# Image stage with the softmax division on two engines and the maximum in two instructions; last stage with four buffers and whole rows (one core)

## The reference, cut to what matters

```python
att = jnp.einsum('bpqhd,bpkhd->bphqk', q_pix * SCALE, k_sel)     # 49 windows, 4 heads, 64 x 256
att = jax.nn.softmax(att, axis=-1)
o = jnp.einsum('bphqk,bpkhd->bpqhd', att, v_sel)
...
xr = mamba(conv(x).reshape(B * H * W, 8, 16)).reshape(B, C, H, W)
g = xr.reshape(B, 4, 32, H, W)
g = (g - g.mean((2, 3, 4))) / jnp.sqrt(g.var((2, 3, 4)) + 1e-5)
return x + silu(g.reshape(B, C, H, W) * gn_w + gn_b)
```

## Time and profile before

| | us |
|---|---|
| median of 3 runs (10958.4 to 10985.89) | 10985.12 |
| the profiled execution | 10976.78 |
| its span | 10974.7 |
| VectorE busy | 9186.9 (84%) |
| TensorE busy | 8590.6 (78%) |
| GpSimd busy | 6007.1 (55%) |
| ScalarE busy | 5945.0 (54%) |

### The profile page before, as it was taken

One profiled execution on the slowest core, in us unless ns is written; L12 is line 12 of the kernel. 1 busy time (PEld: TensorE's weight loads), 2 busy tenths in 40 slices (PEclk: granted clock), 3 DMA queues, 4 the chain that ended last, 5 costly groups with the idle time before them and its releaser, 6 DMA issues. The chain is left out here.

```text
span 10974.7 us, 195169 instructions
## 1 busy us (share of the span) xinstructions
PE 8590.6 (78%) x61658; PEld 3670.2 (33%) x61658; DVE 9186.9 (84%) x11368; ACT 5945.0 (54%) x10997; POOL 6007.1 (55%) x3646
## 2 busy tenths in 40 slices
PE   5888888888888888778777777788777777787850
PEld 3554544544444445222222222222222222222210
DVE  7777777777777777699999999999999999999974
ACT  4555555555555555555555555555555555555533
POOL 2222222222222222487788788887887877878750
PEclk9999999999999999888889898888898888889875
DMA  2222222222222222111111111111111111111139
GB/s 65 66 66 66 66 66 66 66 66 66 66 66 66 66 66 69 43 37 34 36 36 37 35 36 35 37 35 36 36 38 34 38 34 36 36 36 36 35 69 233
DMA packets 865726, 590.60 MB, mean 54 GB/s; under 512 B 622704, under 2 KB 725104, under 8 KB 860496
## 3 DMA queue, kind: packets, MB, share of 16 engines
q1 hardware_dynamic: 761424, 423.61, 17.0%
q0 software_dynamic: 49152, 100.76, 2.5%
q10 hardware_dynamic: 54016, 51.91, 1.6%
HBM read 109.27 MB, written 103.81 MB: 19 GB/s over the span
## 5 line engine op out<-in xcount | busy, mean ns | idle before, releaser
L1136 POOL TENSOR_TENSOR b_hh<-b_hh,b_cn 128x1024 f32<-128x1024 f32 x1600 | 3832.5, 2412 | 1034.3 <-DVE b_hh L1391 1033.4
L1391 DVE TENSOR_TENSOR_SCAN b_hh<-b_dA,b_ub 128x512 f32<-128x512 f32 x3200 | 3864.8, 1208 | 0.0
L1260 ACT ACTIVATE b_dA<-b_db,b_negA 128x448 f32<-128x448 f32 x3200 | 1976.6, 633 | 1736.0 <-PE b_db L1485 1717.8
L267 POOL DMA_DIRECT2D kvsel<-kv x1536 | 1103.0, 721 | 3188.5 <-issue 2408.6
L1383 DVE TENSOR_TENSOR b_ub<-b_ub,b_bn 128x512 f32<-128x512 f32 x3200 | 2173.0, 679 | 360.8 <-PE b_ub L1485 343.8
L1485 PE MATMUL b_ub<-b_rows,b_pick 96*64 96x512 bf16 x6400 | 1401.6, 439 | 988.1 <-DVE b_hh L1391 947.2
L1485 PE MATMUL b_db<-b_rows,b_pick 96*64 96x512 bf16 x6400 | 1266.0, 419 | 218.9 <-ACT b_dA L1260 215.5
L1485 PEld LDWEIGHTS b_ub<-b_rows,b_pick 96*64 96x64 bf16 x6400 | 358.4, 110 | 3172.6 <-DVE b_hh L1391 2523.7
L522 DVE SCALAR_TENSOR_TENSOR oacc<-vpad,vec,oacc 128x1064 f32<-128x1064 f32 (+1 forms) x934 | 1197.9, 1299 | 11.4
L383 ACT ACTIVATE prob<-score,nmax 128x256 f32<-128x256 f32 (+1 forms) x1600 | 735.5, 471 | 818.1 <-DVE nmax L493 726.9
L1521 PE MATMUL b_acc<-b_hh,b_gather 64*32 64x512 f32 x12800 | 1046.1, 716 | 2.8 <-POOL b_hh L1136 2.8
(11 more groups left out here) (179 smaller groups left out, 12057.2 us busy)
## 6 DMA issues: line engine op xcount, KB each, us to landing
b_rows<-b_term SPq DMA_DIRECT2D x2400, 64.0 KB, 2.0
kvsel<-kv SPq DMA_DIRECT2D x1600, 64.0 KB, 2.0
kvsel<-kv POOLq DMA_DIRECT2D x1536, 64.0 KB, 2.0
xpad<-in_x SPq DMA_DIRECT2D x18, 1568.0 KB, 10.6
ys<-ysb ACTq DMA_DIRECT2D x16, 1600.0 KB, 8.6
b_yc<-ys SPq DMA_DIRECT2D x100, 256.0 KB, 2.7
xr<-b_xo SPq DMA_DIRECT2D x100, 256.0 KB, 2.1
x<-x3pad SPq DMA_DIRECT2D x16, 1568.0 KB, 18.1
```

The lines of the kernel that those rows point to most:

```text
L267: eng.dma_start(kvsel[:, slot, j, :, WPIX * t:WPIX * (t + 1)].unsqueeze(1), kv[:, bass.ds(at[t], 1), :, :]).then_inc((s_kv, s_kg)[j][slot] ...
L1136: nc.gpsimd.tensor_tensor(out=now, in0=now, in1=cn[:, par, :].unsqueeze(1).broadcast_to([C, 2, HT]), op=ALU.mult).then_inc(s_pm, 1)
L1260: nc.scalar.activation(later(dA[:, k % DEEP, :]), later(db[k % 2][:, :]), ACT.Exp, scale=negA[:, 8 * q + e:8 * q + e + 1]).then_inc(s_a, 1)
L1391: nc.vector.tensor_tensor_scan(hh[:, k // 2 % PDEEP, HT * (k % 2):HT * (k % 2 + 1)], dA[:, k % DEEP, :], ub[(UNITS * par + k) % 3][:, :], ...
```

## The change

Image stage: `largest` becomes two instructions of two heads each, with a count of the semaphore for each; ScalarE's exponentials wait for the first before head 0 and for the second before head 2. VectorE divides heads 0 and 1; a new function `share` on ScalarE divides heads 2 and 3, by copies with a scale. `turned` is split in two, and the new function stands between the halves. TensorE's transposes wait for both engines. Sequence stage: `xr_dram` is laid out as (128, 4, 12800), so that `store` writes four pieces of 512 B a partition. Last stage: four buffers; xr comes in three loads of whole rows (12,288 B and 12,544 B, and one small); VectorE's body is cut in three, and the moments of image b+1 stand between the scales of image b and its addition.

```diff
@@ layer0, scalar
             def weights(b, p):
                 n, u = b * PAIRS + p, p % 2
-                act.wait_ge(s_m, ONE + n + 1)
                 if p >= 2:
                     act.wait_ge(s_pt, ONE + n - 1)
                 for h in range(HEADS):
+                    if h % 2 == 0:
+                        act.wait_ge(s_m, ONE + 2 * n + h // 2 + 1)
                     nc.scalar.activation(prob[rows(p), u, h], score[rows(p), h, 0:TOPK * WPIX], ACT.Exp,
...
+            def share(b, p):
+                n, u = b * PAIRS + p, p % 2
+                act.wait_ge(s_ri, ONE + n + 1)
+                for h in range(SHARED, HEADS):
+                    now = prob[rows(p), u, h]
+                    m = nc.scalar.activation(now, now, ACT.Copy, scale=rinv[rows(p), u, h:h + 1])
+                m.then_inc(s_ns, 1)
...
                 nc.scalar.activation(pT[:, u, :, rows(p)], turn[:, :, rows(p)], ACT.Copy).then_inc(s_pte, 1)
+            def kept(b, p):
+                n, u = b * PAIRS + p, p % 2
                 act.wait_ge(s_vt, ONE + n + 1)
+                if p >= 2:
+                    act.wait_ge(s_o, ONE + n - 1)
                 nc.scalar.activation(vT[:, u, 0:wins(p)].rearrange("k j c m -> k (j c m)"),
...
                         if p >= 1:
                             turned(b, p - 1)
+                        if p < PAIRS:
+                            share(b, p)
+                        if p >= 1:
+                            kept(b, p - 1)
@@ layer0, vector
-                nc.vector.tensor_reduce(out=nmax[rows(p), u], in_=score[rows(p), :, 0:TOPK * WPIX], axis=AXX, op=ALU.max,
-                                        negate=True).then_inc(s_m, 1)
+                for h in range(0, HEADS, 2):
+                    nc.vector.tensor_reduce(out=nmax[rows(p), u, h:h + 2], in_=score[rows(p), h:h + 2, 0:TOPK * WPIX],
+                                            axis=AXX, op=ALU.max, negate=True).then_inc(s_m, 1)
...
-                for h in range(HEADS):
+                for h in range(SHARED):
@@ layer0, tensor
                         pe.wait_ge(s_nm, ONE + n + 1)
+                        pe.wait_ge(s_ns, ONE + n + 1)
@@ sequences, sync
-                sp.dma_start(xr_dram[bass.ds(n, 1)].rearrange("a c g p -> c (a g) p"), xo[:, :, :]).then_inc(s_os, 16)
+                sp.dma_start(xr_dram[:, :, bass.ds(n * CPX, CPX)], xo[:, :, :]).then_inc(s_os, 16)
@@ normalise
-        S = 2
+        S = 4
...
-                sp.wait_ge(s_res, ONE + FREE + b - 1)
...
+                sp.wait_ge(s_res, ONE + FREE + b - (S - 1))
+                seq = xr_dram[:, g, bass.ds(q * SPX, SPX)]
+                sp.dma_start(xr[0:64, u, 0:PIX - WPIX], seq[0:64, 0:PIX - WPIX]).then_inc(s_x[u], 16)
+                sp.dma_start(xr[0:64, u, PIX - WPIX:PIX], seq[64:128, 0:WPIX]).then_inc(s_x[u], 16)
+                sp.dma_start(xr[64:128, u, :], seq[64:128, WPIX:SPX]).then_inc(s_x[u], 16)
...
+            moments(0, 0, 0)
+            with dve.Fori(0, NB - 1) as q:
+                for g in range(G):
+                    b = q * G + g
+                    scales(b, g)
+                    moments(b + 1, q + (g + 1) // G, (g + 1) % G)
+                    total(b, g)
```

More of the change, by code:

```diff
@@ L189, in layer0 @@
         s_nm = sem("s_nm")
+        s_ns = sem("s_ns")
         s_oa = sem("s_oa")
@@ L239, in layer0 @@
         GROUP = 4
+        SHARED = 2
         def places(k):
@@ L1622, in sem @@
             return sems[-1]
-        red = [ctx.enter_context(nc.psum_tensor(f"c_red{i}", [C, 2], FP32)) for i in range(2)]
-        S = 2
+        red = [ctx.enter_context(nc.psum_tensor(f"c_red{i}", [C, 2], FP32)) for i in range(4)]
+        S = 4
         vec = sb("vec", [C, NV])
@@ L1641, in normalise @@
         s_w = sem("w")
-        s_x = [sem("x0"), sem("x1")]
+        s_x = [sem(f"x{i}") for i in range(S)]
         s_st = sem("st")
@@ L1649, in normalise @@
         s_res = sem("res")
-        s_out = [sem("out0"), sem("out1")]
+        s_out = [sem(f"out{i}") for i in range(S)]
         def v(name):
             return vec[:, _V[name][0]:_V[name][0] + 1]
-        N_W, LOADS, STATS = 2, 6, 9
+        N_W, LOADS, STATS = 2, 5, 9
         FREE = S
@@ L1661, in images @@
                 for g in range(G):
-                    body(q * G + g, q, g, g % 2)
+                    body(q * G + g, q, g, g)
         @block.sync
@@ L1669, in body @@
             def body(b, q, g, u):
-                sp.wait_ge(s_res, ONE + FREE + b - 1)
-                chunk = xr_dram[bass.ds(q * CHUNKS, CHUNKS), :, g, :].rearrange("j c p -> c j p")
-                sp.dma_start(xr[0:64, u, 0:PIX - WPIX].rearrange("c (j p) -> c j p", p=CPX),
-                             chunk[0:64, 0:CHUNKS - 1, :]).then_inc(s_x[u], 16)
-                sp.dma_start(xr[0:64, u, PIX - WPIX:PIX], chunk[64:128, 0, 0:WPIX]).then_inc(s_x[u], 16)
-                sp.dma_start(xr[64:128, u, 0:WPIX], chunk[64:128, 0, WPIX:CPX]).then_inc(s_x[u], 16)
-                sp.dma_start(xr[64:128, u, WPIX:PIX].rearrange("c (j p) -> c j p", p=CPX), chunk[64:128, 1:CHUNKS, :]
-                             ).then_inc(s_x[u], 16)
+                sp.wait_ge(s_res, ONE + FREE + b - (S - 1))
[3 more added lines that the diff above has]
+                sp.dma_start(xr[64:128, u, :], seq[64:128, WPIX:SPX]).then_inc(s_x[u], 16)
                 for two in range(2):
@@ L1720, in body @@
                 act.wait_ge(s_sc, ONE + 3 * b + 3)
-                act.wait_ge(s_out[u], ONE + 32 * (2 * q + g // 2 + 1))
+                act.wait_ge(s_out[u], ONE + 32 * (q + 1))
                 nc.scalar.activation(res[:, u, :], xr[:, u, :], ACT.Silu, bias=shift[:, u], scale=sc[:, u]
@@ L1727, in _ @@
             for x in s_out:
-                act.wait_ge(x, ONE + 32 + 32 * IMGS // 2)
+                act.wait_ge(x, ONE + 32 + 32 * NB)
         @block.vector
@@ L1733, in _, with moments @@
             nc.vector.memset(eps[:, :], EPS_GN)
-            def body(b, q, g, u):
-                dve.wait_ge(s_x[u], ONE + 16 * LOADS * (2 * q + g // 2 + 1))
+            def moments(b, q, u):
+                dve.wait_ge(s_x[u], ONE + 16 * LOADS * (q + 1))
                 for j in range(7):
@@ L1746, in body, with scales @@
                                                in1=mv[:, u, 1:2], op0=ALU.mult, op1=ALU.add).then_inc(s_st, 1)
+            def scales(b, u):
                 dve.wait_ge(s_red, ONE + b + 1)
@@ L1761, in body, with total @@
                                         ).then_inc(s_sc, 1)
+            def total(b, u):
                 dve.wait_ge(s_act, ONE + b + 1)
@@ L1764, in body @@
                                         ).then_inc(s_res, 1)
-            images(dve, body)
+            moments(0, 0, 0)
[5 more added lines that the diff above has]
+                    total(b, g)
+            for g in range(G):
+                b = IMGS - G + g
+                scales(b, g)
+                if g + 1 < G:
+                    moments(b + 1, NB - 1, g + 1)
+                total(b, g)
 TAP_PAIRS = ((0, 1), (2, 3), (None, 0), (1, 2), (3, None))
@@ L1776, in program @@
     ys_dram = nc.dram_tensor("ys", (NB, CHUNKS, C, G, CPX), FP32).ap()
-    xr_dram = nc.dram_tensor("xr", (NB * CHUNKS, C, G, CPX), FP32).ap()
+    xr_dram = nc.dram_tensor("xr", (C, G, NB * SPX), FP32).ap()
     layer0(nc, d, x3_dram, ys_dram)
```

## The result

The changed kernel takes 10787.17 us (median of 4 runs, 10780.03 to 10800.28) against 10985.51 for the kernel before in the same set of runs: ratio 0.9829, 95% interval 0.9808 to 0.9851. It is 198 us faster where 309 were forecast; the time lies inside the range of 10560 to 10820, but outside the stretch of 10600 to 10750 that had the chance of 0.63. The profiled execution took 10800.28 us, span 10798.5, the longest of the four, so that the two profiles differ by 176 us only.

| us | before | after | difference | forecast |
|---|---|---|---|---|
| to the last maximum of the last image | 4317.3 | 4186.1 | −131.2 | −270 |
| from there to the first load of the last stage | 6320.8 | 6317.9 | −2.9 | 0 |
| from that load to the end | 336.6 | 294.5 | −42.1 | −35 |

The account below looks back on a forecast made before the run. No engine is full: a ring of waits bounds the attention loop, DMA engines the last stage. From 10976.8 us, −270 (loop) and −35 (last stage) gave 10672, stated as 10676; range 10560 to 10820, with 0.63 on 10600 to 10750.

Parts of the forecast that it names:

- part 1: Attention loop: two of four divisions move to ScalarE; VectorE −0.72 us a pair, ScalarE +0.80, a copy taken at 0.40.
- part 2: Attention loop: two maxima on VectorE take 1.29 us, +0.08 a pair; the first exponential starts some 0.6 us earlier.
- part 3: Attention loop: ScalarE's new order makes it wait for the reciprocal, and TensorE's transposes wait for both engines; no separate size.
- part 4: Sequence stage: store in 512 B rows takes +0.6 us, 100 times; costed at nothing, up to 60 us without cover.
- part 5: Last stage: whole rows, four buffers, earlier moments; 17.0 us an image against 19.6, tail 29, −35 us in all.
- The ring: Attention loop: chain of waits through TensorE, VectorE and ScalarE over two pairs; 4.45 us a pair instead of 5.185, −270 us.
- The first of the signs named: Attention loop: starts of the maximum would be 4.3 to 4.6 us apart between pairs 2 and 23.
- Rival A: Attention loop: added waits take the gain back, 4.85 us a pair, 10819 us in all; chance 0.17.
- three loads within 10%: Attention loop: work a pair of TensorE 3.93 us, VectorE 4.04, ScalarE 4.13; argument that waits would take the gain back.
- B: Better than forecast: ScalarE's load bounds at 4.13 us a pair, or DMA engines drift; 10539 us or between; chance 0.13.
- C: Attention loop: no change, as ScalarE's copies cost what VectorE's divisions did; break-even at 1.0 us a copy; chance 0.03.
- D: Attention loop: slower, TensorE's clock drops to its lower level, 7.2 us a pair; 11177 with half the pairs; chance 0.04.

Follow-up runs that it names:

- rows_only: Kernel before with only the new xr layout: 512 B store rows, whole-row loads, two buffers, old VectorE order; 10974.54 us, ratio 0.9980.
- merge_late: Changed kernel with VectorE's merge moved from before the division to behind the maxima; 10711.05 us, ratio 0.9747.
- slots4: Changed kernel with four slots for gathered keys and values instead of three; 10750.61 us, ratio 0.9789.
- three_edits_conv_early: Changed kernel with four gather slots, later merge, half of last-stage loads issued by GpSimd, convolution ahead of transposes in three pairs of four; 10556.90 us, ratio 0.9597.

## Why the prediction was right in its sign and short in its size

**Division (part 1) and maxima (part 2): right.** By the groups of the changed kernel (busy us, mean ns of one, then idle time before):

```profile
L397 ACT ACTIVATE prob<-prob,rinv 128x256 f32<-128x256 f32 x768 | 351.2, 512 | 93.5 <-DVE rinv L524 93.4
...
L517 DVE TENSOR_REDUCE nmax<-score 128x2 f32<-128x512 f32 x768 | 493.2, 683 | 301.2 <-PE score L782 299.7
```

A scaled copy takes 0.51 us, but two lie within 0.91 and the next instruction of ScalarE starts 0.80 to 0.82 after the first: 0.40 each, as taken. Two maxima take 1.29, as taken; there is luck in that, as the line for it was drawn through a division (0.35 us) and a maximum (1.21), two different instructions. The first exponential starts 0.72 us after the maximum (1504.95 to 1505.67) instead of 1.23, a gain of 0.5 where I had some 0.6.

**The order on ScalarE and TensorE's new wait (part 3): right in place.** TensorE's idle time before the transposes fell from 397.5 to 243.6 us and is put down to ScalarE.

**The store (part 4): right.** It lands in 2.7 us, as forecast (2.1 in the earlier trace rows), and the time between the images and the last stage is 2.9 us shorter, inside the 5 us named.

```profile
xr<-b_xo SPq DMA_DIRECT2D x100, 256.0 KB, 2.7
```

**The last stage (part 5): right in its total, not in its parts.** First load, first and last statistics, last addition, in answer to the earlier trace rows:

```profile
10504.03 0.59 SPq L1698 DMA_DIRECT2D c_xr<-xr  x1
...
10521.56 1.15 DVE L1760 BATCH_NORM_STATS2 c_stats<-c_xr 128x6 f32<-128x448 f32 x2 [16.64 <-DMA c_x<-x]
...
10770.09 3.78 DVE L1760 BATCH_NORM_STATS2 c_stats<-c_xr 128x6 f32<-128x448 f32 x7 [4.40 <-DMA c_x<-x]
...
10785.44 3.42 DVE L1787 TENSOR_TENSOR c_res<-c_res,c_x 128x3136 f32<-128x3136 f32 x1 [3.77 <-ACT c_res L1744]
```

Steps of 16.57 us (17.0 forecast) and a tail of 28.4 (29). The split inside was off: whole rows gave 1.9 us an image instead of 1, buffers and order 1.15 (17.72 to 16.57) instead of the 1.6 that the sum had left for them, and that the two errors offset is luck. By the rule of the Trainium skill (DMA: Bandwidth & Descriptors, Specifications) that I had weighed there, 512 B being enough for line rate, rows alone would have given nothing. `rows_only` gave 29.5 us of the stage, so here the trace disagrees by more than the windows of the earlier trace rows had shown, with the one small load less left open.

**The sum for the attention loop: the term that failed.** The ring was taken at 4.45 us a pair, saving 0.735; it saved 0.31. The step of the text that failed is "Merges make single steps uneven; I take 4.45": merges were given 0.04 us a pair. They measured 0.27 a pair of pairs 2 to 23 (`merge_late`; 0.21 if the 76 us of the medians are spread over 368 steps), since each stands between the `lepe` steps and the reciprocal. The second is the waits for gathered keys, which the text named as what would make it wrong and gave no term: 0.12 a pair (`slots4`; 0.10 by the medians). They grew from 21.6 to 72.1 us, so that by its own sign the prediction of the loop was wrong. I had computed a shorter step and left the gathers at their old cover. Both taken out, the loop takes 110.7 us an image and the step is 4.566; my 23 x 0.735 would have made 109.6. So these two edits win 8.1 of the 9.2 us an image that were missing. The rest is open, 1.1 us of the loop: the steps of pairs 2 to 23 are still 0.12 longer than 4.45, and the other steps make up for some of it. Hand-overs between the engines, which the sum took at 0.1 us for two pairs, are a candidate that no run measured. The first of the signs named failed too: the maxima start 4.906 apart and not 4.3 to 4.6.

**Rival A** (4.85 a pair, 10819) was nearer than the forecast (10676), in the loop and in the time, 4.906 even passing it. Its headline, that waits take the gain back, is what came. Of its arguments, three loads within 10% was not the cause: `merge_late` and `slots4` change no load and win 0.27 and 0.12 of the missing 0.46. The new waits that it named are in the trace (TensorE for ScalarE's copies 243.6 us, ScalarE for the reciprocal 93.4), and no run takes away one of them alone. The merges and the gathers it did not name. The three loads come near to being the limit only at the end, in `three_edits_conv_early`, where ScalarE is busy 95% of a stretch of 4.32 us a pair. B, C and D did not come; the granted clock in the loop stayed at 0.98.

## What to carry to other kernels

When a ring gets shorter by a computed amount, look at what stands in front of each of its steps in the queue of that engine, not only at the sums of busy time: work of 0.75 us every fourth pair cost about 1 us each time, and reordering it gave 76 us. Every prefetch with a fixed number of slots has a cover that shrinks with the step: give it a term of its own. An edit that gives nothing alone may be worth much once the wait that it feeds is gone: moving the convolution gave no gain on the changed kernel and 96 us on the one with four slots and the later merge, so read which wait grew before it is dropped.

## What the runs showed of the hardware

Loads of 64 partitions go faster when SP and GpSimd issue one half each than when SP issues both, 241 to 250 against 213 to 219 GB/s alone and 322 against 287 with stores, at about the same DMA share of 1.0. The Trainium skill (DMA: Bandwidth & Descriptors, Rules for kernel authors) says that spreading transfers over issuing engines doesn't help bandwidth, as all run on the same 16 DMA engines; the measurement here says otherwise for halves of 64 partitions. Whether it is the second queue or which halves meet in time was not told apart.

Two scaled copies of 128x256 on ScalarE took 0.91 us and one 0.51. The Trainium skill (ScalarE: Activation LUTs, What ACT_TABLE_LOAD costs) gives about 280 ns + 0.833 ns an element for an instruction with one operand of a value a partition, as the scale is here, and an overlap of 93 ns between neighbours. That makes an estimate of 0.49 us for one and 0.89 for two; the trace agrees within 0.02.

The sequence stage, in which no kernel changed anything but the layout of the store, took between 6075 and 6116 us from first to last scan. It goes by sets: 6075 to 6092, 6090 to 6100 and 6103 to 6116 us in the three sets of experiments, in which the median of the kernel before was 10985.6, 10992.5 and 10996.4. So differences of ten or twenty us between single profiles of different sets are not to be put down to an edit.
